# Three float32r products of high and low parts in place of float32 in four projections of a decoder, with weights split by GpSimd for every pair

## What is computed

```python
def _mha(s, t, kv_w, q_w, o_w, o_b, mask):          # 16 heads of 64
    k, v = jnp.split(s @ kv_w, 2, axis=-1)
    q = t @ q_w
    scores = jnp.where(mask == 0, -1e9, einsum(q, k) * 64 ** -0.5)
    return softmax(scores) @ v @ o_w + o_b
def step(t, p):                                      # six times
    tn = _ln(t, norm_g, norm_b)
    t = _mha(tn, tn, skv, sq, sow, sob, self_mask) + t
    tn = _ln(t, norm_g, norm_b)
    t = _mha(ctx, tn, ckv, cq, cow, cob, ctx_mask) + t
    tn = _ln(t, pg, pb)
    return t + relu(tn @ w1 + b1) @ w2 + b2          # w1: 256 x 1024
```

## Time and profile before

| | us |
|---|---|
| median of 3 executions | 2963.3 (2961.9 to 2964.0) |
| the profiled execution, its own time | 2966.0 |
| its span, first to last instruction | 2964.2 |
| TensorE busy (two records for each float32 product) | 2843.4, 96% |
| VectorE busy | 1678.4, 57% |
| ScalarE busy | 1301.7, 44% |
| GpSimd busy | 963.7, 33% |
| DMA traffic | 120.7 MB, mean 41 GB/s |

### The profile page before, as it was taken

The page is one execution under the profiler, slowest core; times in us unless marked ns, Lnnn a source line. Parts: engine busy times, 40 slices in busy tenths (PEclk is TensorE's granted clock), DMA queues, the critical chain, the costliest instruction groups (busy, mean ns, idle before and its releaser), DMA issues.

```text
span 2964.2 us, 69078 instructions
## 1 busy us (share of the span) xinstructions
PE 2843.4 (96%) x23656; PEld 2313.3 (78%) x23656; DVE 1678.4 (57%) x6361; ACT 1301.7 (44%) x4273; POOL 963.7 (33%) x1169
## 2 busy tenths in 40 slices
PE   6778999999999999999999999999999999999999
PEld 4656887887887887887887887877887878878877
DVE  2443664664655654654655655655655655655655
ACT  2223543544543543544544444444544544444444
POOL 1002432432332332333333333333333333333333
PEclk9988999999999999999999999999999999999999
DMA  5003101113101123001023011033011033011010
GB/s 175 1 1 99 27 3 29 26 64 101 22 9 29 21 69 101 16 15 28 13 77 101 7 23 29 3 87 101 1 28 29 1 88 91 12 29 29 2 28 14
DMA packets 132260, 120.69 MB, mean 41 GB/s; under 512 B 15261, under 2 KB 121318, under 8 KB 130278
## 3 DMA queue, kind: packets, MB, share of 16 engines
q1 hardware_dynamic: 131942, 116.53, 15.2%
HBM read 115.59 MB, written 0.92 MB: 39 GB/s over the span
## 4 chain that ended last, share of the span: by engine, by line
issue 48%; POOL 25%; PE 21%; DVE 2%; ACT 2%; POOLq 1%; DMA 0%; SPq 0%; DVEq 0%; ACTq 0%
POOL prob L555 18%; PE proj L595 8%; PE proj L615 3%; POOL prob L525 3%; PE sum L615 3%; PE sum L786 2%; POOL ctx_parts L546 1%; PE proj L587 1%; POOL tw L503 1%; PE score L762 1%; PE tr L773 1%; DVE qcT L1216 1%; PE sum L595 1%; PE score L595 1%; POOLq L554 1%
## 5 line engine op out<-in xcount | busy, mean ns | idle before, releaser
L555 POOL TENSOR_TENSOR prob<-prob,rtotal 128x375 f32<-128x375 f32 x672 | 543.4, 812 | 761.0 <-DVE rtotal L1489 760.0
L981 ACT ACTIVATE prob<-prob,negmax 128x375 f32<-128x375 f32 (+1 forms) x686 | 417.7, 609 | 451.9 <-DVE negmax L1480 422.9
L904 PE MATMUL sum<-pT,ctx 32*128 32x224 f32 (+1 forms) x4608 | 500.7, 358 | 12.8 <-DVE qcT L1472 12.8
L904 PE MATMUL tr<-pT,ctx 32*128 32x224 f32 (+1 forms) x4608 | 500.6, 358 | 0.0
L904 PEld LDWEIGHTS sum<-pT,ctx 32*128 32x128 f32 (+1 forms) x4608 | 417.8, 185 | 73.4 <-issue 73.4
L1480 DVE CUSTOM_DVE_ANT_0 prob<-score,cbias 128x375 f32<-128x375 f32 x672 | 357.1, 531 | 195.0 <-PE score L595 193.4
L904 PEld LDWEIGHTS tr<-pT,ctx 32*128 32x128 f32 (+1 forms) x4608 | 417.0, 185 | 0.0
L595 PE MATMUL score<-ctx_parts,qc_high 128*128 128x376 f32 x1344 | 411.9, 387 | 0.0
L1498 DVE STREAM_TRANSPOSE pT<-prob 128x384 f32<-128x384 f32 x672 | 372.8, 558 | 0.0
L525 POOL TENSOR_TENSOR prob<-prob,rtotal 112x448 f32<-112x448 f32 x200 | 186.6, 933 | 543.5 <-DVE rtotal L1348 543.5
L1054 ACT ACTIVATE prob<-prob,negmax 112x112 f32<-112x112 f32 x800 | 298.9, 377 | 84.9 <-DVE negmax L1366 84.9
(11 more groups left out here) (224 smaller groups left out, 4754.0 us busy)
## 6 DMA issues: line engine op xcount, KB each, us to landing
ctx<-ctx SPq DMA_DIRECT2D x192, 176.0 KB
w_kv<-sa_kv SPq DMA_DIRECT2D x6, 2048.0 KB, 9.8
f<-ff_w SPq DMA_DIRECT2D x12, 1024.0 KB, 8.6
cmask<-ctx_mask SPq DMA_DIRECT2D x24, 375.0 KB, 4.3
w_q<-sa_q SPq DMA_DIRECT2D x6, 1024.0 KB, 11.0
w_o<-sa_ow SPq DMA_DIRECT2D x6, 1024.0 KB, 5.5
c_q<-ca_q SPq DMA_DIRECT2D x6, 1024.0 KB, 8.7
c_o<-ca_ow SPq DMA_DIRECT2D x6, 1024.0 KB, 11.1
```

The costliest lines, as they stand in the source:

```text
L555: pool.tensor_tensor(row, row, rtotal[:, G * SG + i:G * SG + i + 1].broadcast_to([P, S2]), ALU.mult).then_inc(prob_ready, 1)
L904: ins = pe.matmul(bank[:, 0:HT * R], ctx4[keys_of, m // (HALVES // NB), j, :], pT[keys_of, m % 2, :, j * R:(j + 1) * R], start=j == 0, sto ...
L981: act.activation(o, i, ACT.Exp, bias=negmax[0:rows, col:col + 1], scale=scale, accum_out=total[0:rows, col:col + 1]).then_inc(exp_ready, 1)
```

## The change

The float32 products of values, self queries, cross queries and first feed-forward are each replaced by three float32r products accumulated in the same bank: high tokens with high weights, high tokens with low weights, low tokens with high weights. Keys, the outputs and the sums stay as they are, and so does the start's first pair.

The weights are split by GpSimd with `cut`: a copy of 128 x 256 to float32r (high part) and a subtraction (low part) that overwrites the raw weights. CUTS is 8 per weight matrix; four matrices give 32 cuts a pair. w_v and w_q share one place (`w_vq`, high part and raw or low part), c_q and f_1 another (`w_cf`), so each of the four is loaded again for every pair. The tokens are split by VectorE (`parts_of_normed`), three times a pair. SP's order is new, and all five streams are unrolled.

```diff
+    CUT = 256
+    CUTS = EK * HDIM // CUT
+    Q_CUT_STEPS = range(1, 1 + CUTS)
+    F_CUT_STEPS = range(12, 12 + CUTS)
-        w_q = sb("w_q", [P, EK, HDIM])
-        w_kv = sb("w_kv", [P, EK, 2 * HDIM])
-        c_q = sb("c_q", [P, EK, HDIM])
-        f_1 = sb("f_1", [P, EK, FC * P])
+        w_vq, w_vq_parts = in_one_place("w_vq", "w_vq_parts", [P, 2, EK, HDIM])
+        w_cf, w_cf_parts = in_one_place("w_cf", "w_cf_parts", [P, 2, EK, HDIM])
+        w_k = sb("w_k", [P, EK, HDIM])
...
@@ block.sync
+            for it in range(L * PAIRS):
+                at = Place(MAIN_LOOP, it)
+                l, p = it // PAIRS, it % PAIRS
+                next_layer, layer_after = (min((it + n) // PAIRS, L - 1) for n in (1, 2))
+                next_p = (p + 1) % PAIRS
+                new_layer = p == PAIRS - 1 and l < L - 1
+                if new_layer:
...
+                sp.wait_ge(ready["proj1"], at.at("proj1", SA_OUT + 1 + V2))
+                load_w_q(next_layer)
+                sp.wait_ge(smask_used, it + 1)
+                load_pair_smask(next_p)
+
+                sp.wait_ge(ready["sum1"], at.at("sum1", 1 + HALF))
+                load_f_1(l)
...
+                sp.wait_ge(ready["proj1"], at.at("proj1", Q_END))
+                load_w_v(layer_after)
+                if p == PAIRS - 2 and l < L - 1:
+                    load_w_k(l + 1)
 
                 sp.wait_ge(ready["proj1"], at.at("proj1", CA_OUT + 1))
+                load_pair_cmask(next_p)
+
+                sp.wait_ge(ready["proj1"], at.at("proj1", FF_OUT))
+                load_c_q(next_layer)
+                if new_layer:
+                    load_ca(l + 1)
+                    load_c_o(l + 1)
+                load_pair_ctx4(next_p)
...
@@ block.gpsimd
+            def cut(at, name, i, times):
+                raw, parts = (w_vq, w_vq_parts) if name in ("w_v", "w_q") else (w_cf, w_cf_parts)
+                k, cols = i % EK, slice(i // EK * CUT, (i // EK + 1) * CUT)
+                if i == 0:
+                    pool.wait_ge(loaded[name], times * 16)
+                pool.tensor_copy(parts[:, 0, k, cols], raw[:, 1, k, cols]).then_inc(pool_step, 1)
+                pool.wait_ge(pool_step, at.at("pool", at.next("pool") + 1))
+                pool.tensor_tensor(parts[:, 1, k, cols], raw[:, 1, k, cols], parts[:, 0, k, cols].bitcast(f32), ALU.subtract)\
+                    .then_inc(cut_ready[name], 1)
...
                     pool.tensor_tensor(tw[:, :, :], t_all[:, ds(p * NB, NB), :],
                                        o_bias[:, 0, :].unsqueeze(1).broadcast_to([S, NB, E]), ALU.add).then_inc(resid_ready, 1)
+                    for i in range(CUTS // 2, CUTS):
+                        cut(at, "w_v", i, it + 1)
...
                         .then_inc(split_ready, 1)
+                    for i in range(CUTS - 2):
+                        cut(at, "c_q", i, it + 1)
                     inverse_std(at, 0)
+                    for i in range(CUTS - 2, CUTS):
+                        cut(at, "c_q", i, it + 1)
...
                                            ALU.mult).then_inc(prob_ready, 1)
+                        if i in Q_CUT_STEPS:
+                            cut(at, "w_q", i - Q_CUT_STEPS[0], it + 2)
+                        if i in F_CUT_STEPS:
+                            cut(at, "f_1", i - F_CUT_STEPS[0], it + 1)
...
                     normalise_group(at, 7)
+                    for i in range(CUTS // 2):
+                        cut(at, "w_v", i, it + 2)
...
@@ block.tensor
+            def projected_in_parts(at, name, w, high, low, c):
+                cols = slice(c * P, (c + 1) * P)
+                project(at, name, [w[:, n, k, cols] for n in (0, 1, 0) for k in range(EK)],
+                        [m[:, k, :] for m in (high, high, low) for k in range(EK)])
...
+            def first_projected_in_parts(at, names, w, high, low, k_low):
+                opened = [fill(at, name) for name in names]
+                for part, a in ((0, high), (1, high), (0, low)):
+                    if a is low:
+                        pe.wait_ge(tn_low_ready, k_low)
...
+                    pe.wait_ge(tn_high_ready, at.at("tn_high", 1))
                     emptied(at, "sum0")
                     weights("c_kT")
                     for n in range(0, HC + 4, 2):
                         if n < HC:
-                            projected(at, "sum0", c_q, tnT, n)
-                            projected(at, "sum1", c_q, tnT, n + 1)
+                            pe.wait_ge(cut_ready["c_q"], it * CUTS + (n + 2) * CUTS // HC)
...
@@ block.scalar, in normed
+                    if to_parts:
+                        ins.then_inc(tn_full_ready, 1)
+                if to_parts:
+                    act.wait_ge(tn_full_ready, EK * at.at("tn_high", at.next("tn_high") + 1))
+                    act.sem_inc(taken[name], 1)
...
@@ block.vector
+            def parts_of_normed(at, full, high, low):
+                done = at.at("tn_high", at.next("tn_high") + 1)
+                for k in range(EK):
+                    dve.wait_ge(tn_full_ready, EK * (done - 1) + k + 1)
+                    ins = dve.tensor_copy(high[:, k, :], full[:, k, :])
+                ins.then_inc(tn_high_ready, 1)
+                gate(tn_high_ready, done)
+                dve.tensor_tensor(low[:, :, :], full[:, :, :], high[:, :, :].bitcast(f32), ALU.subtract).then_inc(tn_low_ready, 1)
...
                     values(at, 0)
+                    parts_of_normed(at, tnT_full_1, tnT_high, tnT_low_1)
                     values(at, 1)
                     new_smask(it + 1)
```

More of the change, by code:

```diff
@@ L249, in attention_layers @@
         fwv = [a[:, 2 * EK * E + E:FW] for a in fw]
-        f1_flat, f2_flat, co_flat, cq_flat, wo_flat, kT_flat = (
-            a[:, :, :].rearrange("p k n -> p (k n)") for a in (f_1, f_2, c_o, c_q, w_o, kT))
+        f2_flat, co_flat, wo_flat, kT_flat = (a[:, :, :].rearrange("p k n -> p (k n)") for a in (f_2, c_o, w_o, kT))
+        f1_flat, cq_flat = (w_cf[:, n, :, :].rearrange("p k n -> p (k n)") for n in range(2))
         low_0, low_1 = before_low[:, 0, :], before_low[:, 1, :]
@@ L299, in attention_layers @@
         loaded = {n: sem(f"{n}_loaded") for n in
-                  ("w_q", "w_kv", "w_o", "c_q", "c_kT", "c_v", "c_o", "f_1", "f_2", "small", "sa_ob", "ca_ob")}
+                  ("w_q", "w_k", "w_v", "first_w_v", "w_o", "c_q", "c_kT", "c_v", "c_o", "f_1", "f_2", "small", "sa_ob", "ca_ob")}
         dve_step = sem("dve_step")
@@ L315, in attention_layers @@
         high_ready = sem("high_ready")
+        tn_full_ready = sem("tn_full_ready")
+        tn_high_ready = sem("tn_high_ready")
+        tn_low_ready = sem("tn_low_ready")
+        cut_ready = {n: sem(f"{n}_cut_ready") for n in ("w_v", "w_q", "c_q", "f_1")}
         stored = sem("stored")
@@ L1107, in _ @@
             at.check()
-            with act.Fori(0, L) as l:
-                with act.Fori(0, PAIRS) as p:
+            for l in range(L):
+                for p in range(PAIRS):
                     at = Place(MAIN_LOOP, l * PAIRS + p)
@@ L1422, in _ @@
             at.check()
-            with dve.Fori(0, L) as l:
-                with dve.Fori(0, PAIRS) as p:
+            for l in range(L):
+                for p in range(PAIRS):
                     it = l * PAIRS + p
```

189 lines of the change are left out of this document (107 added, 82 removed).

## The result

The changed kernel takes 3305.7 us (median of 4, 3304.5 to 3307.4) against 2963.2 beside it: 342 us more, ratio 1.116, 95% interval 1.114 to 1.118. The forecast was 3385, range 3060 to 3560.

What follows compares the result with a forecast made beforehand. TensorE, busy 96%, was taken as the bound. Per pair, -4.1 gain, +7.9 norm, +1.4 and +1.5 clock, +4.9 mask, +5.5 loop and +0.35 copy made +17.4 us, times 24 +419: 3385 us, range 3060 to 3560.

Steps and rivals of the forecast that it cites:

- W1: Before the first norm: ten cuts ahead of GpSimd's variance step make TensorE wait 7.9 us a pair at the transposes.
- W2: TensorE's clock at half after waits: +1.4 us a pair at values(3), +1.5 in cross queries behind the mask's wait.
- W3: Cross queries: the self mask, now loaded behind w_q, arrives late and TensorE waits 4.9 us a pair.
- W4: Loop of 28 steps: GpSimd's sixteen cuts between rows delay the sums, TensorE waits about 5.5 us a pair.
- f_1's second half: Before f_1: VectorE copies the second half behind ScalarE, +0.35 us a pair.
- TensorE's gain: Float32r products in 24 chunks and 4 values banks save TensorE 4.1 us a pair.
- The cut: GpSimd's copy (0.40 us), gap (0.19) and subtraction (0.69) for one weight piece: 1.28 us, bounds 1.03 to 1.32.
- what it saves counts until another engine is late for it: TensorE, busy 96% of the span, is the bound; its savings shorten the kernel until another engine is late.
- The cuts beside VectorE: Before the cross queries: GpSimd cuts during VectorE's normalising lengthen it through shared ports, 0.5 us a pair within W1.
- only the first place counts: Rival: only the wait before the first norm costs; mask and loop cuts stay hidden; +5.2 us a pair, 3091 us, chance 0.12.
- faster: Rival: GpSimd's cut costs far less, 0.65 us or under, so only the mask's wait remains; 2936 us, chance 0.05.
- the slow narrow product: Rival: float32r products with 224 columns take 0.378 us as in float32; +44.6 us a pair, 4037 us, chance 0.08.

Runs made afterwards that it cites:

- e6: e5 with one c_q cut ahead of the inverse deviations and the other seven behind VectorE's normalised rows: 2931.7 us, ratio 0.990 to the kernel before.
- e8: e6 with the first product of two of the four values banks issued twice: 2934.9 us, ratio 0.991.
- e11: e6 without the product of low weights and high rows in all four projections, cuts and waits kept: 2885.6 us, ratio 0.974.
- e5: Changed kernel with e1's and e2's moves, f_1 cuts behind the loop, four w_q cuts ahead of it, four behind rows 9, 11, 13, 15: 2941.9 us, ratio 0.993.
- e1: Changed kernel with the next pair's mask load issued ahead of the wait for values(3) and of w_q: 3181.5 us, ratio 1.074.
- e3: Changed kernel with the eight w_q cuts moved ahead of the 28-step loop and the eight f_1 cuts behind it: 3224.6 us, ratio 1.088.
- e10: e6 with all eight w_q cuts behind every other loop row, 1 to 15, none ahead of the loop: 2938.3 us, ratio 0.991.
- e2: Changed kernel with the inverse deviations ahead of all eight c_q cuts, not behind six: 3170.4 us, ratio 1.070.
- e12: Changed kernel with the moves of e1 and e2 together, loop left as the change has it: 3018.8 us, ratio 1.019.
- e9: e6 with GpSimd's context parts moved behind the c_q cuts and three of these cuts, not one, ahead of the inverse deviations: 2930.1 us, ratio 0.989.

## Why the prediction was right, by its steps

The direction, the size and all three places were as forecast. The terms can be measured against e6, in which the three waits are gone and which does the same work; before to e6 then gives the gain. Per pair:

| term | forecast | measured | from |
|---|---|---|---|
| W1, wait for the norm | +7.9 | +5.96 | T, after less e6 |
| W2, clock at values(3) | +1.4 | +1.28 | Q, after less e6 |
| W3 and W2, mask and clock | +6.4 | +5.40 | S, after less e6 |
| W4, loop | +5.5 | +3.44 | loop, after less e6 |
| f_1's second half | +0.35 | +0.33 | F, after less before |
| TensorE's gain | -4.1 | -2.16 | T, Q, S, loop, end: e6 less before |
| sum | +17.4 | +14.2 | |

24 pairs by 14.2 make 341 of the 342 us. The forecast's excess of 3.2 us a pair is made of waits 5.2 too long and a gain 1.9 too large, which partly cancel: that 3385 came within 79 us of 3306 is in part luck, for with the gain right it would have been some 125 over.

**The cut** was priced at 1.28 us by a line through the rows and is 1.155 from start to start. The copy's 0.40 was exact, the subtraction is 0.73 for 0.69, but the hand-over between the two is 0.08 and not the 0.19 of the earlier trace rows, and the next cut's copy starts before the record of the last subtraction ends. Ten cuts ahead of the norm are 1.25 us less: veps starts at 15.4 after TensorE's first values product, forecast 16.6; the 2.3 us from there to the transposes (1673.87 to 1676.20) were forecast as 2.37.

**W1** lost another 0.65 on the other side: TensorE could not have been at the transposes at 11.1, but at 11.75. **W4**: row 0 starts 3.22 us after the first scores (1694.94 to 1698.16), as forecast; row and cut take 1.93 for 2.09, the third sum starts at 39.5 us for 41.3, and what it takes longer, 3.4 us, stays to the end of the loop. **W3**: from w_q's issue to the bias pass 5.17 us (1679.80 to 1684.97), forecast 5.9; TensorE idles 3.1 in this pair, 3.4 in the mean, forecast 4.9. **W2**: the mean clock is 0.952, forecast 0.95.

**TensorE's gain** is in proportion the term that was off by most, 2.2 us for 4.1. There are two causes, a chunk that saves less than forecast and saved time that becomes waiting.

The first is the price of a chunk in its place. Steps of the loop with a chunk of keys in float32 in the kernel before (first fence; a step with a chunk of queries takes the same there), and with a chunk of queries in the changed kernel (second), in order of time:

```profile
1529.15 0.66 PE L595 MATMUL score<-ctx_parts,qc_high 128*128 128x376 f32 x2
...
1529.82 0.92 PE L595 MATMUL proj<-tnT_next,w_kv 128*128 128x224 f32 x4
1530.42 0.66 PE L595 MATMUL score<-ctx_parts,qc_high 128*128 128x376 f32 x2
```

```profile
1719.37 0.60 PE L652 MATMUL proj<-tnT_next_high,w_vq_parts 128*128 128x224 f32 x4
1719.81 0.39 PE L652 MATMUL proj<-tnT_next_low,w_vq_parts 128*128 128x224 f32 x2
1720.03 0.52 PE L652 MATMUL score<-ctx_parts,qc_high 128*128 128x376 f32 x2
...
1721.23 0.51 PE L652 MATMUL score<-ctx_parts,qc_high 128*128 128x376 f32 x2
```

Four narrow products start within 0.44 us and two within 0.22: 0.110 each, forecast 0.107; four of 512 columns from 1668.27 to 1669.19 are 0.230 each, as forecast. But what counts is the distance from one step's first score to the next: 1.27 us with the float32 chunk (1529.15 to 1530.42) and 1.20 with the new one (1720.03 to 1721.23). A chunk saves 0.07 us there and not 0.114. Two cross chunks with what follows them take 1.53 us in e6 (1833.64 to 1835.17) and 1.71 before (1408.81 to 1410.52), 0.09 less each. The loop is 0.56 shorter in e6 than before and the end 0.62, where eight chunks in each were to save 0.91. TensorE idles hardly more there than before, 0.61 instead of 0.53 us in the loop and 0.13 instead of 0.10 in the end (medians), so in both the shortfall is the price and not a wait.

The Trainium skill ("TensorE: Matmul & The Clock Gate", Back-to-back issue gap) has a formula that makes 96 ns at 224 columns, an estimate, and says itself that it is too low for few columns in a stream with weight loads; the 0.110 measured is above it. It is nearer to what the Trainium skill gives on the same page (LDWEIGHTS) for loading 128 columns of weights, 107 ns, also an estimate.

The second is a step of the prediction that failed: "what it saves counts until another engine is late for it". I did not ask which engine is late next. It is VectorE at once: in the kernel before its normalisation ended at 1513.74 and TensorE's transposes started at 1513.86, so the chain of other engines stood 0.12 us ahead of TensorE already. From the end of the output rows TensorE waits for statistics, inverse deviations, normalising, and then for the high and low parts, a chain that the change makes longer. Of the 1.0 us saved ahead of the transposes 0.4 arrives. At the cross queries nothing of 0.9 does (S +0.08 in e6): the first four chunks, with the waits, take 3.57 us instead of 3.12, and the other four give 0.37 back. Q, on the other hand, is 0.66 shorter for the 0.34 forecast, because in the kernel before TensorE also idled 0.40 us there for VectorE's copy of the values, which e6 no longer shows. For the stretch up to the first scores e8 and e11 show the same from both sides: two products more cost 3 us instead of 11, and with 7.1 us of products less in each pair a pair is only 1.9 shorter.

Two readings of the recorded working are slightly off, without effect on the forecast: 0.61 less 0.51 is 0.10 and not 0.11, and half of 0.189 is 0.0945, which makes the largest saving 6.25 instead of 6.5 and the lower end 3032 instead of 3026.

**The cuts beside VectorE** were to cost W1 0.5 us, by the earlier trace rows; e5 and e6 measure 0.53. The rule of the Trainium skill that VectorE and GpSimd take the shared ports in turn ("SBUF — State Buffer", Who interferes with whom) agrees with that.

**The rivals.** Of them, "only the first place counts" is refuted by e1 and e3, which undo the other two and gain 124 and 81 us; "faster" by the cut's 1.155 us; and the slow narrow product by 0.110.

e6 keeps some longer pairs, up to 115 us for 110, each the first pair of a layer. In them the mask still stands behind the loads of the new layer, as the row of one shows:

```profile
1609.91 0.68 DVE L1452 TENSOR_SCALAR sbias<-smask 112x224 f32<-112x224 int32 x1 [2.21 <-DMA smask<-self_mask]
```

The kernel before has such pairs too; no run moved these loads.

## What to carry to other kernels

Work given to an engine with idle time is priced by its place in that engine's order: the same 32 cuts cost 14 us a pair in one order and let the kernel win 1.3 in another. Give each piece a deadline (who reads it, when) and put it behind everything with an earlier one; between urgent short steps put single pieces (e5, e10), though these runs do not show whether the spacing or the smaller number did it. And before counting a saving on the busiest engine, read at each of its stages who hands it the next operand: where a chain of other engines stands close behind, the saving becomes a wait, and a wait can cost more than its length. Price a saving by the distance from one step to the next and not by the product alone.

## What the runs showed of the hardware

- TensorE's clock went to half behind waits shorter than I had reckoned with: in e11 TensorE idles about 1.5 us ahead of the transposes in nearly every pair, and in 14 of the 24 pairs the clock is then at half for 6.8 us or more (0.51 over the stretch shown). With 0.44 us there (e6) the whole run stands at 0.991.
- The stretch at half behind the mask's wait is 3.4 us in 18 of the 24 pairs of the changed kernel (wait 3.4 us in the mean, another wait just before) and in 14 pairs of e2 (wait 3.8, the other one gone). In the rest it is 6.8 or 10.2. Removing both waits gave 27 us more than the two removals singly (e12), so the clock's cost of two waits isn't the sum of each alone.
- A dependent pair on GpSimd has only 0.08 us between the end of one and the start of the next at 256 columns (1673.11 to 1673.19), 0.19 at 750.
- The profile's releaser can be a neighbour of the real one: in e9 it names a cut that had ended 2.9 us earlier, in a wait that several semaphores guard.
